# Recurrent layer: the diagonals of the state's pieces laid out with the sequences innermost

## What is computed

```python
def _L0_cond_ref(x, h0, Wx, Wh, b):
    xW = x @ Wx + b                      # all time steps
    def step(h, xw_t):
        h = tanh(xw_t + h @ Wh)          # [16, 128] @ [128, 128]
        return h, h
    # 128 steps, each needs the state of the one before
    ...
x = x + attn(L0_cond(x, cond))           # state space layer (mamba)
x = x + ffn(L0_cond2(x, cond))           # gru, quantized ffn
x = x + gla(L1_cond(cond, x))            # gated linear attention
x = x + moe(L1_cond2(x, cond))           # lstm, mixture of experts
```

## Time and profile before

| what | value |
| --- | --- |
| median of 3 runs | 9069.2 us (9068.93 to 9073.12) |
| the profiled execution's own time | 9070.96 us |
| its span, first to last instruction | 9069.2 us |
| of this `rnn` | about 5560 us, 128 time steps, 41.4 us from one to the next |
| PE busy / PEld / DVE / ACT / POOL | 6612.7 / 2651.3 / 7509.4 / 4347.2 / 1508.4 us |
| mean granted clock of TensorE | 0.878 |

### The profile page before, as it was taken

The page is one execution under the profiler, slowest core; times in us unless marked ns, Lnnn a source line. Parts: engine busy times, 40 slices in busy tenths (PEclk is TensorE's granted clock), DMA queues, the critical chain, the costliest instruction groups (busy, mean ns, idle before and its releaser), DMA issues. The chain is left out here.

```text
span 9069.2 us, 110790 instructions
## 1 busy us (share of the span) xinstructions
PE 6612.7 (73%) x34945; PEld 2651.3 (29%) x35217; DVE 7509.4 (83%) x12442; ACT 4347.2 (48%) x4172; POOL 1508.4 (17%) x1495
## 2 busy tenths in 40 slices
PE   4777777777777777777777776288888887662779
PEld 1222323232323232323232322022222222331443
DVE  5899999999999999999999997799999998336223
ACT  3565656565656665666666564133333332112222
POOL 0000000000000000000000000177777775000000
PEclk7888888888888888888888887599999999996999
DMA  0000000000000000000000000000000000000000
GB/s 6 1 1 1 1 1 1 1 1 1 1 1 1 1 1 1 1 1 1 1 1 1 1 1 8 29 4 4 4 3 3 3 3 4 0 5 3 3 14 5
DMA packets 14004, 28.01 MB, mean 3 GB/s; under 512 B 3665, under 2 KB 11602, under 8 KB 12434
## 3 DMA queue, kind: packets, MB, share of 16 engines
q1 hardware_dynamic: 13586, 22.47, 0.9%
HBM read 15.12 MB, written 7.34 MB: 2 GB/s over the span
## 5 line engine op out<-in xcount | busy, mean ns | idle before, releaser
L897 POOL TENSOR_TENSOR hc<-hh,cg 128x512 f32<-128x512 f32 x1024 | 1294.4, 1267 | 513.4 <-DVE hh L880 513.4
L825 ACT ACTIVATE ps_m<-ps_m,aneg 128x508 f32<-128x508 f32 x1024 | 673.4, 658 | 1192.0 <-DVE hh L880 1067.7
L880 DVE TENSOR_TENSOR_SCAN hh<-ps_m,bx 128x512 f32<-128x512 f32 x1024 | 1236.1, 1212 | 0.0
L796 PE MATMUL ps_m<-hc,pick 128*128 128x512 f32 x2048 | 1053.1, 598 | 2.1 <-POOL hc L897 0.8
L507 DVE TENSOR_TENSOR_SCAN co<-rh_d 128x3088 f32<-128x3088 f32 x128 | 843.8, 6592 | 254.6 <-ACT rh_d L368 254.6
L230 POOL TENSOR_TENSOR t<-gs,minus 128x176 f32<-128x176 f32 x128 | 72.6, 567 | 5072.1 <-DVE gs L156 5072.1
L507 DVE TENSOR_TENSOR_SCAN co<-rx_d 128x772 f32<-128x772 f32 x544 | 915.4, 1746 | 0.0
L260 PE MATMUL r_ps<-rh_diag,whq 32*128 32x512 bf16 x3072 | 353.3, 624 | 767.6 <-DVE rh_diag L126 767.0
L862 DVE TENSOR_TENSOR bx<-ps_m,bg 128x512 f32<-128x512 f32 x1024 | 678.6, 668 | 50.3 <-PE ps_m L809 50.1
L252 PE MATMUL r_ps<-wdiag,xsp 32*128 32x512 bf16 x3312 | 348.5, 581 | 487.3 <-ACT rx_d L368 452.5
L398 ACT ACTIVATE rh_pd<-r_ps 128x512 f32<-128x512 f32 x512 | 264.6, 603 | 900.7 <-PE r_ps L260 900.7
(11 more groups left out here) (392 smaller groups left out, 11565.1 us busy)
## 6 DMA issues: line engine op xcount, KB each, us to landing
rows_scratch<-pc SPq DMA_DIRECT2D x48, 128.0 KB
rows<-rows_scratch SPq DMA_DIRECT2D x128, 48.0 KB
ew<-in_e SPq DMA_DIRECT2D x3, 1024.0 KB, 6.9
co<-in_x_dn SPq DMA_DIRECT2D x1, 1024.0 KB, 4.8
xcur<-in_x_dn SPq DMA_DIRECT2D x1, 1024.0 KB
out_x<-xcur SPq DMA_DIRECT2D x1, 1024.0 KB, 3.9
qi<-in_f_q SPq DMA_DIRECT2D x1, 384.0 KB, 3.1
xpw<-in_xp_t SPq DMA_DIRECT2D x1, 257.0 KB
```

The source lines that it names most:

```text
L796: e.matmul(ps[:, 6, :], pick[:, 128 - un:256 - un], hc[un % NHC][:], start=False, stop=True, skip_group_check=True).then_inc(summed, 1)
L825: e.activation(da[un % NDA][:, :, 1:T], ps[:, un % 2, :].rearrange("p (n t) -> p n t", n=NG4)[:, :, 1:T], ACT.Exp, scale=aneg[:, 0:1]).the ...
L880: e.tensor_tensor_scan(hh[un % NBUF][:], da[un % NDA].rearrange("p n t -> p (n t)"), bx[un % NBUF][:], 0.0, ALU.mult, ALU.add).then_inc(sc ...
L897: e.tensor_tensor(hc[un % NHC][:], hh[un % NBUF][:], cg[:], ALU.mult).then_inc(weighted, 1)
```

## The change

The diagonals are laid out the other way round: k outside, the 16 sequences n innermost. The identity is held in full, as `idn`, 32 x 16 elements of bf16 per partition, made once by a VectorE copy from `id32`; VSETUP counts one more operation. `diagonal(q)` is now a tensor_tensor with both inputs and the output in bf16, whose inner step is one element in all three. `h_mov` still hands TensorE the columns in the order (n, k), so that PSUM and everything behind it stay as they were; it now reads them from memory at 32 bytes (16 elements of bf16) from one column to the next, and moves on by 2 bytes after every 32 columns. No instruction of the time steps is added, removed or moved.

```diff
@@ -57,7 +57,7 @@
         ps = ctx.enter_context(nc.psum_tensor("r_ps", [128, 8, 512], F32))
 
         negid = sb("negid", [128, 128])
-        id32 = sb("id32", [128, KB])
+        id32 = sb("id32", [128, KB]); idn = sb("idn", [128, KB, N], BF16)
         wx = sb("wx", [128, D]); wh = sb("wh", [128, D])
         whq = sb("whq", [128, 3, D], BF16); wxq = sb("wxq", [128, 3, D], BF16)
         wdiag = sb("wdiag", [128, 3, D, KB], BF16)
@@ -73,7 +73,7 @@
             return f
         R, X = side("rh_"), side("rx_")
         R.update(part=sb("rh_part", [128, 3, N], BF16), rest=sb("rh_rest", [128, 2, N]),
-                 diag=sb("rh_diag", [128, 3, N, KB], BF16), gain=sb("rh_gain", [128, N, D]),
+                 diag=sb("rh_diag", [128, 3, KB, N], BF16), gain=sb("rh_gain", [128, N, D]),
                  sg=sb("rh_sg", [128, 2, NB, 512], BF16))
         co = sb("co", [128, N * LX])
         ends = co[:].rearrange("p (n l) -> p n l", l=LX)[:, :, LX - 1]
@@ -109,7 +109,7 @@
         NXC = 4
         KXC = NXC + 1
         V0 = 1
-        VSETUP = 57
+        VSETUP = 58
 
         class Tally:
 
@@ -123,8 +123,8 @@
         def pieces(tl, e, F, src, dep=None):
 
             def diagonal(q):
-                return tl.inc(e.tensor_tensor(F["diag"][:, q], id32[:].unsqueeze(1).to_broadcast([128, N, KB]),
-                                              F["part"][:, q, :].unsqueeze(2).to_broadcast([128, N, KB]), ALU.mult))
+                return tl.inc(e.tensor_tensor(F["diag"][:, q], idn[:], F["part"][:, q, :].unsqueeze(1).to_broadcast([128, KB, N]),
+                                              ALU.mult))
             if dep is not None:
                 tl.wait(dep)
             i = tl.inc(e.tensor_tensor(F["part"][:, 0, :], src, nought[:], ALU.add))
@@ -296,7 +296,7 @@
                         ins.then_inc(re_mm, 1)
 
             h_stat = lambda b, q: whq[rows(b), q, :]
-            h_mov = lambda b, r: R["diag"][rows(b), r].rearrange("p n k -> p (n k)")
+            h_mov = lambda b, r: R["diag"][rows(b), r].rearrange("p k n -> p n k")
             h_diff = lambda b: R["gain"][:, :, KB * b:KB * (b + 1)]
             x_diff = lambda b: piece(X, "pd", b)
             xp_stat = lambda b, q: xsp[rows(b), q, :]
@@ -459,6 +459,8 @@
             for b in range(2, NB):
                 tl.wait(i)
                 i = tl.inc(e.tensor_tensor(id32[:], id32[:], ident[:, KB * b:KB * (b + 1)], ALU.add))
+            tl.wait(i)
+            tl.inc(e.tensor_copy(idn[:], id32[:].unsqueeze(2).to_broadcast([128, KB, N])))
             tl.inc(e.memset(xpc[:, :, T * N:], 0.0))
             for src, dst in ((wx[:], wxq), (wh[:], whq), (xt, xpc)):
                 n = D if dst is not xpc else T * N
```

## The result

The changed kernel takes 11,635.2 us as the median of 4 runs (11,633.6 to 11,635.6), the kernel before 9,071.1 in the same comparison. The ratio is 1.2826 (95% interval 1.2804 to 1.2849). The prediction had the sign and the term, but 10,736 us; its range ended at 11,200.

The account below looks back on a forecast made before the run. Bound: the path from diagonal 0 through TensorE and ScalarE's last pieces to scan and tanh. L281 7.29 us later plus L287's 5.72 gave 13.01 per step, 1665 over 128, on 9070.96: 10,736 us; range 9,450 to 11,200.

Parts of the forecast that it names:

- the sign: Whole kernel: the change makes it slower, chance 0.85, against faster 0.13 and same 0.02.
- the term: TensorE's diagonal reads at 32 bytes from column to column decide the result: 0.853 us per 512 columns, chance 0.50.
- What bounds the kernel: Time step's path: diagonal 0, TensorE to L294, ScalarE's last pieces, scan, tanh, next diagonal; VectorE at both ends only.
- VectorE's packing: VectorE's three diagonals per step take 421 ns each for 687; diagonal 0, on the path, gains 0.27 us.
- The price of a far column: TensorE's reads of the diagonals cost 1.67 ns per column, 0.853 us per 512, at either level of its clock.
- half rate: Rival: TensorE's memory gives one far access in 0.83 ns; 3.2 us more per step, 9,481 us, chance 0.17.
- two cycles: Rival: two array cycles per column at either clock level, product slowed too; 5.8 us per step, 9,810 us, chance 0.05.
- no cost: Rival: TensorE's far reads are free and packed diagonals gain 35 to 47 us; 9,030 us, chance 0.13.
- The clock: Rival: slow columns delay TensorE's high level; L272 3.4 us more per step, about 11,180 us and more, chance 0.12.
- L272 keeps its length: TensorE's f32 matmuls behind the product take as long as before: 0 us more.
- L281 and L284 read f32 side by side and keep their time: TensorE's f32 matmuls between L275 and L287, not reading far columns: 0 us more.
- as before: L294, ScalarE's L368, the scan and the tanh follow L287 with no time added of their own.

Follow-up runs that it names:

- The dense kernel: The changed kernel with TensorE reading all diagonals side by side in memory order, numbers wrong, VectorE's packed diagonals kept: 9,067.4 us, ratio 0.9997.
- the pairs: The kernel before with its own diagonal layout, made in bf16 from state parts written twice side by side: 9,066.5 us, ratio 0.9996.
- the block of steps: The kernel before with a measuring block in front, TensorE reading constant operands at different steps: 0.917 us per group of four at 32 bytes.

## Why the prediction was wrong, by its steps

- **What bounds the kernel**: right. The excess sits on TensorE's way from diagonal 0 to L294, and the scan's wait for ScalarE's L368 grew from 2.0 to 20.2 us per step (forecast some 13).
- **VectorE's packing**: the size was right, 421 ns and -0.28 us at diagonal 0. Its worth was wrong: the step held that 0.27 us on the path are 0.27 us per step. The dense kernel, the pairs and the change with the f32 identity show 0 to 0.04% for it, because the clock's return doesn't come sooner. The prediction had that return "during the product". Its own put it later: a clock of 0.84 over 12.5 us is (1 - 0.84) / 0.5 x 12.5 = 4.0 us at the low level, until about 2511.5, which is 0.2 us into L272. So the product lay wholly ahead of the return, and L272 was the first to pay for anything that happened to it.
- **The price of a far column**: the right choice between bounds, taken from VectorE's rows, and 7% too small: 1.79 ns for 1.67. On 23 groups that is 3.09 + 5.59 + 6.30 - 2.58 - 4.98 - 5.72 = 1.70 us per step, 218 us. The rivals "half rate", "two cycles" and "no cost" fell with the block of steps: 0.917 us at either level of the clock (the levels: the windows of the step shown above). That steps of 8 bytes cost nothing is so for VectorE's f32 row from which it was read, and not for TensorE's bf16 columns (0.453 us against 0.216).
- **The clock**: here the forecast failed. The step "L272 keeps its length", "L281 and L284 read f32 side by side and keep their time" and L294 "as before" should have been L272 2.12, L281 2.41, L294 and its surroundings 1.13 longer, 5.66 us per step, 725 us. It stood as a rival with a chance of 0.12, priced for L272 alone (3.4 us, 11,180) and with L281 and L284 (12,060). Its sign was right and its place in part: L272 and L281 slowed down, L284 didn't, and L294, which it had not named, did. The measured 11,635 lies between the two. What was said against it, that the array stays occupied, was no evidence: the earlier trace rows could have told only of gaps, since no row of before has slow columns, and so the two cases should have stood far closer together and the range should have reached to 12,060.
- The sum: 13.01 + 1.70 + 5.66 = 20.37, measured 20.36 for the step shown. Over all steps the mean is 20.06 us, since the kernel before loses some 2.8 us on every eighth step, the first of a turn, where L281 waits for VectorE's L500, and the changed one doesn't.

## What to carry to other kernels

Let TensorE's bf16 columns lie at most 4 bytes apart, or in runs of four and more: packing a VectorE operation by a layout that another engine must read at 16 bytes or more moves the cost to the engine that reads most often, here 24 groups against 3 operations. At 8 bytes the price is already double. If a run of length two is enough for VectorE, as here, pack with doubled operands and leave the layout alone. Behind a stretch of bf16 columns 12 bytes or more apart expect matmuls at the low clock, and where the clock changes level within a step, don't count a fraction of a microsecond as won before a run shows it.

## What the runs showed of the hardware that I had not expected

- TensorE's clock fell to 1.2 GHz in stretches without any gap: with bf16 columns 12 bytes and more apart (0.676 us per group and more). It held in the stretches at 8 bytes (0.453), with pairs at 32 bytes (0.459) and with f32 columns at 16 bytes (0.900 per instruction).
- TensorE's price for the step is the same at 1.2 and 2.4 GHz (0.916 in L260, 0.917 in L275), and near VectorE's 1.67 ns; weights at 32 bytes cost nothing visible in the pitch (L159: 0.216).
- Steps of the recurrent loop can take up small gains and losses whole: 0.27 us sooner or later at the product changed 9,069 and 11,635 us by no more than their scatter, and a turn of eight steps took 491.5 us in the change whether the diagonals took 421 or 686 ns.
